# Second normalisation of the first two batches: logarithm and exponential on ScalarE, rows scaled on VectorE

## The chip, the cores and the metric

One core of a Trainium2 chip runs the whole kernel. Five engines (TensorE, VectorE, ScalarE, GpSimd and SyncE, in the profile PE, DVE, ACT, POOL and SP) each run a program of their own, in order, and meet at semaphores. The metric is the device time of one execution in microseconds; the median of several is compared. Lower is better.

## What is computed

x is 8 batches of 256 tokens of 128 values, float32. A cross attention with 8 heads of 16, then a mixture of 8 experts, two chosen for each token:

```
x = x + xattn(layernorm(x), ctx, ctx, W_Q, W_K, W_V, W_O)   # softmax over the heads' axis (axis=1)
x = x + ffn(layernorm(x), Wr, br, W1, b1, W2, b2)
layernorm(x) = (x - mean) / sqrt(var + 1e-5)
logits = x @ Wr + br;  gates = softmax over the two largest
h = relu(x @ W1[e] + b1[e]);  out = sum_e gates[e] * (h @ W2[e] + b2[e])
```

The second `layernorm` feeds the router and the experts. It is the one that the change touches.

## The kernel before

A batch's 256 tokens are two tiles (t = 0, 1) of 128 rows. The batches run through a software pipeline: while the experts of one batch run on TensorE, the scores and softmax of the next are made by VectorE and ScalarE. The attention of a batch is four units (u = 0 to 3) of 128 x 1024 scores. Every engine's order is written out by hand: `beginning()` lists the steps up to the middle of batch 1's experts one by one, and `period(i)` repeats the steady pattern after that. An engine does nothing out of this order, so a wait holds up all that stands behind it.

The steps that matter, with their lines:

- `head_max(b, u)` (VectorE, L904) takes the maximum over heads of a unit, `subtract_max` (TensorE, L344) subtracts it, `exponentiate` (ScalarE, L643) makes `e_sb`.
- `head_sum(b, u)` sums `e_sb` over the heads: on TensorE for batch 0 (L352), on GpSimd afterwards, as `half_sum`, `quarter_sum`, `e_sum` (L1156, L1158, L1161). `invert_sum` (ScalarE, L652 and L654) takes the reciprocal as a logarithm and an exponential, and `normalize` (VectorE, L912) makes `attn`.
- `add_residual(b)` (VectorE, L857) makes `x1`. `ln2(b)` (VectorE, L864 to L872) makes the mean, `ln2_var` (variance plus epsilon) and `ln2_neg`. `ln2_end(b)` (GpSimd, L1167 and L1170) makes `ln2_rstd` as a power of -0.5 and `ln2_off` = -mean * rstd. `make_x1n(b)` (ScalarE, L610) scales and shifts the two tiles into `x1n`; the profile shows it under L597, the helper `normalise`.
- `transpose_x1n` (TensorE, L283) transposes `x1n`; it waits for `x1n_made` and for the bank in `misc_ps`, for batch 1 until `k_lo(4)` has read it. `take_x1T_hi` (ScalarE, L594) and `x1T_low` (VectorE, L876) split the result into a high and a low part, and `route` (TensorE, L299) and `expert_up(b, 0)` (TensorE, L404) wait for the low part.
- `expert_up(b, e)` (L404), `relu` (ScalarE, L671), `expert_down` (TensorE, L417) and `add_expert` (VectorE, L978) run an expert. `y_ps` has two banks, so `expert_down(b, e)` waits until `add_expert(b, e - 2)` is over.

In the profile's names digits and some endings are left out: `ln2_var` and `ln1_var` are both `ln_var`, `x1` is `x`.

The orders around the change, in the lists of `beginning()`:

- VectorE, batch 0: `add_residual(0)`, `ln2(0)`, `head_max(1, 2)`, `head_max(1, 3)`, `x1T_low(0)`, `normalize(1, 0)`. Batch 1: `head_max(2, 3)`, `add_residual(1)`, `ln2(1)`, `add_expert(0, 3)`, `normalize(2, 0)`, `k_lo(4)`, `head_max(3, 0)`, `x1T_low(1)`, `add_expert(0, 4)`, `add_expert(0, 5)`, `take_logits(1)`.
- ScalarE, batch 0: `invert_sum(1, 0)`, `take_v(2)` (the profile's `v_pad`), `make_x1n(0)`, `take_x1T_hi(0)`, `exponentiate(1, 2)`, `relu(0, 0)`. Batch 1: `exponentiate(2, 2)`, `relu(0, 5)`, `invert_sum(2, 1)`, `take_k_hi(4)`, `make_x1n(1)`, `relu(0, 6)`, `take_x1T_hi(1)`.
- GpSimd: `head_sum(1, 0)`, `ln2_end(0)`, `head_sum(1, 1)` and so on; `head_sum(2, 1)`, `ln2_end(1)`, `split_w1(7)`, `head_sum(2, 2)`.
- TensorE: `transpose_x1n(0)`, `subtract_max(1, 2)`, `expert_up(0, 0)`, `scores(2, 0)`, `route(0)`. Batch 1: `expert_up(0, 6)`, `expert_down(0, 5)`, `transpose_x1n(1)`, `subtract_max(2, 3)`, `expert_up(0, 7)`, `route(1)`, `expert_down(0, 6)`.

Of the kernel before, what the change touches and what calls it, by code (L numbers as in the profile page):

```python
# [9 lines left out]
ALU = mybir.AluOpType  # L10
ACT = mybir.ActivationFunctionType
AX = mybir.AxisListType

P = 128
# [3 lines left out]
def build(nc, x, ctx_t, w_attn, wr, br, w1, b1_t, w2, b2, out):  # L18
# [3 lines left out]
    TT = S // P  # L22
# [8 lines left out]

    PERIODS = B + 5
    B2_AFTER = 2
    PE_SUMS = 4

    with ExitStack() as stack:
        def sb(name, shape, dt=F32):
            return stack.enter_context(nc.sbuf_tensor(name, shape, dt))
# [4 lines left out]
        def sem(name):  # L43
            return stack.enter_context(nc.semaphore(name))
# [47 lines left out]
        x1 = sb("x1", [P, TT, D])  # L92

        ln2_stats = sb("ln2_stats", [P, TT, 6])
        ln2_mv = sb("ln2_mv", [P, TT, 2])
        ln2_var = sb("ln2_var", [P, TT])
        ln2_rstd = sb("ln2_rstd", [P, TT])
        ln2_neg = sb("ln2_neg", [P, TT])
        ln2_off = sb("ln2_off", [P, TT])
        x1n = sb("x1n", [P, TT, D])  # L100
# [48 lines left out]
        ln2_step, ln2_var_made, ln2_neg_made, ln2_rstd_made, ln2_off_made, x1n_made = (  # L149
            sem("ln2_step"), sem("ln2_var_made"), sem("ln2_neg_made"), sem("ln2_rstd_made"), sem("ln2_off_made"),  # L150
            sem("x1n_made"))
        x1T_done, x1T_hi_made, x1T_lo_made = sem("x1T_done"), sem("x1T_hi_made"), sem("x1T_lo_made")
        logits_done, logits_step, logits_made, router_step, gap_made, gap_exp_made, gates_made = (
            sem("logits_done"), sem("logits_step"), sem("logits_made"), sem("router_step"), sem("gap_made"), sem("gap_exp_made"),
# [7 lines left out]
        def wait(eng, semaphore, n):  # L162
            if n > 0:
                eng.wait_ge(semaphore, n)
# [4 lines left out]
        def summed_on_pe(n):  # L169
            return n < PE_SUMS  # L170

# [90 lines left out]
        def _(pe):  # L262
# [125 lines left out]
            def expert_up(b, e):  # L388
# [3 lines left out]
                if j == 0:  # L392
                    pe.wait_ge(log_made, PE_SUMS)
                if b == 0:
# [196 lines left out]
        def _(act):  # L591
# [4 lines left out]
            def normalise(dst, src, off, rstd, t):  # L596
                return nc.scalar.activation(dst, src, ACT.Identity, bias=off[:, t:t + 1], scale=rstd[:, t:t + 1])  # L597
# [6 lines left out]
                op.then_inc(xn_made, 1)  # L604

            def make_x1n(b):
                act.wait_ge(ln2_off_made, b + 1)
                wait(act, x1T_done, b)
                for t in range(TT):
                    op = normalise(x1n[:, t, :], x1[:, t, :], ln2_off, ln2_rstd, t)  # L610
                op.then_inc(x1n_made, 1)
# [33 lines left out]
            def invert_sum(b, u):  # L645
# [4 lines left out]
                else:  # L650
                    act.wait_ge(sum_made, n + 1 - PE_SUMS)
                    nc.scalar.activation(log_sum[:, u, :], e_sum[:, u, :], ACT.Ln).then_inc(log_made, 1)  # L652
# [27 lines left out]
            def period(i):  # L680
                kv, coming, now, f, g, old = i, i - 1, i - 2, i - 3, i - 4, i - 5
                if there(g):
                    make_x1n(g)
# [47 lines left out]
            def beginning():  # L731
# [30 lines left out]
                invert_sum(1, 0)  # L762
                take_v(2)
                make_x1n(0)
                take_x1T_hi(0)
                exponentiate(1, 2)
# [21 lines left out]
                invert_sum(2, 1)  # L788
                take_k_hi(4)
                make_x1n(1)  # L790
                relu(0, 6)
                take_x1T_hi(1)
# [41 lines left out]
        def _(dve):  # L834
# [26 lines left out]
            def ln2(b):  # L861
                dve.wait_ge(x1_made, b + 1)
                for t in range(TT):
                    op = nc.vector.bn_stats(ln2_stats[:, t, :], x1[:, t, :])  # L864
                op.then_inc(ln2_step, 1)
                dve.wait_ge(ln2_step, 2 * b + 1)
                for t in range(TT):
                    op = nc.vector.bn_aggr(ln2_mv[:, t, :], ln2_stats[:, t, :])
                op.then_inc(ln2_step, 1)
                dve.wait_ge(ln2_step, 2 * b + 2)  # L870
                nc.vector.tensor_scalar(ln2_var[:], ln2_mv[:, :, 1], EPS, None, ALU.add).then_inc(ln2_var_made, 1)  # L871
                nc.vector.tensor_scalar(ln2_neg[:], ln2_mv[:, :, 0], -1.0, None, ALU.mult).then_inc(ln2_neg_made, 1)  # L872

            def low_part(dst, src, hi, hi_made, n, made):
# [90 lines left out]
            def add_expert(b, e):  # L965
# [3 lines left out]
                if e == 0:  # L969
                    dve.wait_ge(gates_made, b + 1)  # L970
                if e == B2_AFTER + 1:
                    dve.wait_ge(b2_added, b + 1)
# [10 lines left out]
            def add_b2(b):  # L983
                dve.wait_ge(b2_done, b + 1)
                dve.wait_ge(gated, E * b + B2_AFTER + 1)
                nc.vector.tensor_tensor(acc[:].rearrange("p t d -> p (t d)"), misc_ps[:, 0:S],
                                        acc[:].rearrange("p t d -> p (t d)"), ALU.add).then_inc(b2_added, 1)

            def period(i):
# [35 lines left out]
                if there(f):  # L1025
                    ln2(f)
# [109 lines left out]
        def _(pool):  # L1136
# [14 lines left out]
            def head_sum(b, u):  # L1151
                n = UNITS * b + u
                at = 2 * (n - PE_SUMS)
                pool.wait_ge(exp_made, n + 1)
# [7 lines left out]
                                        ALU.add).then_inc(sum_made, 1)  # L1162

            def ln2_end(b):
                pool.wait_ge(ln2_var_made, b + 1)
                wait(pool, x1n_made, b)
                nc.gpsimd.tensor_tensor(ln2_rstd[:], ln2_var[:], neg_half[:, 0:TT], ALU.pow).then_inc(ln2_rstd_made, 1)  # L1167
                pool.wait_ge(ln2_rstd_made, b + 1)
                pool.wait_ge(ln2_neg_made, b + 1)
                nc.gpsimd.tensor_tensor(ln2_off[:], ln2_neg[:], ln2_rstd[:], ALU.mult).then_inc(ln2_off_made, 1)  # L1170

            def split_w1(e):
# [93 lines left out]
```

## Time and profile before

| | us |
|---|---|
| median of 3 runs | 211.2 |
| lowest and highest of them | 210.09, 212.29 |
| the profiled execution, in all | 212.29 |
| its span, first to last instruction | 210.4 |

The span is what the profile's rows are measured in: time 0 is its start. Busy time of TensorE's matmuls is 199.6 us of it, VectorE 167.7, ScalarE 132.3, GpSimd 112.8. Matmuls are pipelined and their ends are modelled, so the first figure is no measure of TensorE at its peak. The mean granted TensorE clock is 0.992 of full speed. In a row, "L876" is a line of the kernel, `out<-in` are the tiles by name, "128x256 f32" partitions and elements in a row, and what stands in brackets is idle time of the engine just before, with what ended it.

### The profile page before, as it was taken

What the parts mean: (1) busy time and instruction counts of PE and PEld (TensorE: products, weight loads), DVE (VectorE), ACT (ScalarE), POOL (GpSimd) and SP (SyncE); (2) the same over time, 40 slices, a digit from 0 to 9 for tenths busy, and PEclk for the clock granted to TensorE, in tenths of its full rate; (3) what the DMA queues carried; (4) which work ended last, traced back from release to release, by engine and by line L of the source; (5) the groups of instructions that cost most, each with busy time, mean ns of one, the idle gap of its engine ahead of it and who ended that gap; (6) DMA issues with size and microseconds to landing.
All of it is one profiled execution on the core that took longest, in us unless ns stands there. A gap on an engine that the chain in (4) does not pass through costs nothing.

```text
span 210.4 us, 4952 instructions
## 1 busy us (share of the span) xinstructions
PE 199.6 (95%) x1736; PEld 176.7 (84%) x1736; DVE 167.7 (80%) x453; ACT 132.3 (63%) x316; POOL 112.8 (54%) x132
## 2 busy tenths in 40 slices
PE   6999977698999999999999999999999999999994
PEld 6845865596799978997999889998998899789993
DVE  6388859878798999899888988898999888556532
ACT  2227738678577856877677767587757776345441
POOL 8502838849976397719662856466746674010000
PEclk9999999979999999999999999999999999999999
DMA  6649586805605163315041503332001000000000
GB/s 182 149 121 273 145 258 183 247 4 163 171 19 166 37 174 99 94 34 154 2 153 51 171 7 121 83 126 50 3 0 28 0 2 0 28 3 2 25 3 25
DMA packets 20248, 18.70 MB, mean 89 GB/s; under 512 B 1760, under 2 KB 18688, under 8 KB 20224
## 3 DMA queue, kind: packets, MB, share of 16 engines
q1 hardware_dynamic: 17472, 16.91, 27.9%
q10 hardware_dynamic: 2752, 1.48, 2.8%
q8 instruction: 14, 0.23, 0.5%
q14 instruction: 10, 0.08, 0.1%
HBM read 11.83 MB, written 6.55 MB: 87 GB/s over the span
## 4 chain that ended last, share of the span: by engine, by line
PE 91%; DVE 3%; issue 2%; ACT 2%; POOL 1%; DVEq 0%; POOLq 0%; ACTq 0%
PE y_ps L417 28%; PE h_ps L404 22%; PE score_ps L344 7%; PE misc_ps L363 6%; PE score_ps L332 6%; PE h_ps L352 3%; PE score_ps L265 3%; PE misc_ps L384 2%; PE score_ps L321 2%; PE score_ps L404 2%; PE misc_ps L372 1%; PE misc_ps L270 1%; PE misc_ps L310 1%; PE misc_ps L289 1%; PE misc_ps L283 1%
## 5 line engine op out<-in xcount | busy, mean ns | idle before, releaser
L671 ACT ACTIVATE hT<-h_ps,b_sb 128x256 f32<-128x256 f32 x118 | 49.4, 470 | 34.1 <-PE h_ps L404 33.0
L417 PE MATMUL y_ps<-w_sb,hT 128*128 128x128 f32 x512 | 68.5, 277 | 0.0
L417 PEld LDWEIGHTS y_ps<-w_sb,hT 128*128 128x128 f32 x512 | 63.3, 191 | 3.4 <-issue 2.2
L1156 POOL TENSOR_TENSOR half_sum<-e_sb 128x512 f32<-128x512 f32 x28 | 37.2, 1328 | 32.0 <-ACT e_sb L643 31.7
L912 DVE TENSOR_TENSOR attn<-e_sb,e_rcp 128x1024 f32<-128x1024 f32 x32 | 42.2, 1321 | 3.3 <-ACT e_rcp L654 3.3
L904 DVE TENSOR_REDUCE shift_m<-score_ps 128x128 fp32r<-128x1024 f32 x32 | 38.7, 1213 | 4.0 <-PE score_ps L332 2.8
L404 PE MATMUL h_ps<-x1T_hi,w_lo 128*128 128x256 f32 x118 | 38.1, 323 | 1.3 <-ACT hT L671 0.6
L643 ACT ACTIVATE e_sb<-score_ps 128x1024 f32<-128x1024 f32 x32 | 32.8, 1024 | 5.6 <-PE score_ps L344 5.4
L978 DVE SCALAR_TENSOR_TENSOR acc<-y_ps,gates,acc 128x128 f32<-128x128 f32 x96 | 29.1, 343 | 8.6 <-PE y_ps L417 7.3
L404 PE MATMUL h_ps<-x1T_hi,w_hi 128*128 128x256 f32 x118 | 33.3, 283 | 0.0
L404 PE MATMUL h_ps<-x1T_lo,w_hi 128*128 128x256 f32 x118 | 33.3, 282 | 0.0
L1158 POOL TENSOR_TENSOR quarter_sum<-half_sum 128x256 f32<-128x256 f32 x28 | 27.5, 983 | 2.2
L404 PEld LDWEIGHTS h_ps<-x1T_hi,w_lo 128*128 128x128 f32 x118 | 22.6, 192 | 4.2 <-issue 2.0
L404 PEld LDWEIGHTS h_ps<-x1T_lo,w_hi 128*128 128x128 f32 x118 | 22.6, 192 | 0.3
L404 PEld LDWEIGHTS h_ps<-x1T_hi,w_hi 128*128 128x128 f32 x118 | 22.6, 191 | 0.0
L332 PE MATMUL score_ps<-q_stack,k_stack 128*128 128x256 f32 x112 | 20.0, 303 | 1.9 <-issue 1.9
L344 PE MATMUL score_ps<-shift_m,neg_ident 128*128 128x512 f32 x64 | 21.8, 421 | 0.0
L1161 POOL TENSOR_TENSOR e_sum<-quarter_sum 128x128 f32<-128x128 f32 x28 | 17.6, 629 | 2.2
L332 PEld LDWEIGHTS score_ps<-q_stack,k_stack 128*128 128x128 f32 x112 | 15.4, 194 | 2.4 <-issue 2.3
L1167 POOL TENSOR_TENSOR ln_rstd<-ln_var,neg_half 128x2 f32<-128x2 f32 x8 | 5.7, 707 | 21.0 <-DVE ln_var L871 21.0
L363 PE MATMUL misc_ps<-attn,v_pad 128*32 128x256 f32 x256 | 15.5, 382 | 0.6 <-issue 0.6
L344 PEld LDWEIGHTS score_ps<-shift_m,neg_ident 128*128 128x128 f32 x64 | 10.1, 193 | 3.1 <-issue 2.8
(112 smaller groups left out, 286.3 us busy)
## 6 DMA issues: line engine op xcount, KB each, us to landing
k_scratch<-k_parts SPq DMA_DIRECT2D x14, 256.0 KB, 2.6
k_stack<-k_scratch SPq DMA_DIRECT2D x14, 256.0 KB, 3.9
q_stack<-q_scratch SPq DMA_DIRECT2D x28, 128.0 KB, 2.7
q_scratch<-q_parts SPq DMA_DIRECT2D x7, 256.0 KB, 2.1
w_sb<-in_w SPq DMA_DIRECT2D x1, 1024.0 KB, 7.1
out_y<-y_out SPq DMA_DIRECT2D x8, 128.0 KB, 1.9
x_all<-in_x ACTq DMA_DIRECT2D x1, 768.0 KB, 6.1
ctxT<-in_ctx_t SPq DMA_DIRECT2D x1, 640.0 KB, 5.1
```

The costliest lines, as they stand in the source:

```text
L332: mm = nc.tensor.matmul(score_ps[:, u % 2, 2 * j * P:(2 * j + 2) * P], k_stack[:, b % 2, j, kt * P:(kt + 1) * P], q_stack[:, b % 2, j, :, ...
L344: mm = nc.tensor.matmul(score_ps[:, u % 2, half * BANK:(half + 1) * BANK], neg_ident[:], m4, start=False, stop=True, skip_group_check=True)
L363: mm = nc.tensor.matmul(misc_ps[32 * g:32 * g + 32, 0:S], v_pad[:, b % 4, kt, h, :], attn[:, b % 2, kt, h, :], start=(odd == 0 and kt == 0 ...
L404: mm = nc.tensor.matmul(hidden(j)[:, c * S:(c + 1) * S], w[:, e, c * P:(c + 1) * P], xt[:, b % 2, :], start=(k == 0), stop=(k == 2))
L417: mm = nc.tensor.matmul(y_ps[:, j % 2, t * D:(t + 1) * D], hT[:, j % 2, c, t * P:(t + 1) * P], w2_sb[:, e * HC + c, :], start=(c == 0), st ...
L643: nc.scalar.activation(e_sb[:, u, :], score_ps[:, u % 2, :], ACT.Exp, scale=SCALE).then_inc(exp_made, 1)
L671: op = nc.scalar.activation(hT[:, j % 2, c, :], hidden(j)[:, c * S:(c + 1) * S], ACT.Relu, bias=b1_sb[:, e * HC + c:e * HC + c + 1])
L904: nc.vector.tensor_reduce(shift_m[:, u % 2, :], score_ps[:, u % 2, :].rearrange("p (h q) -> p q h", h=H), AX.X, ALU.max).then_inc(max_made, 1)
L912: nc.vector.tensor_tensor(attn[:, b % 2, kt, :, qt * P:(qt + 1) * P], e_sb[:, u, :].rearrange("p (h q) -> p h q", h=H), e_rcp[:, u, :].uns ...
L978: op = nc.vector.scalar_tensor_tensor(out=dst, in0=y_ps[:, j % 2, t * D:(t + 1) * D], scalar=gates[:, b % 2, t, e:e + 1], in1=src[:, t, :] ...
L1156: nc.gpsimd.tensor_tensor(half_sum[:], e[:, 0:HQ // 2], e[:, HQ // 2:HQ], ALU.add).then_inc(sum_step, 1)
L1158: nc.gpsimd.tensor_tensor(quarter_sum[:], half_sum[:, 0:HQ // 4], half_sum[:, HQ // 4:HQ // 2], ALU.add).then_inc(sum_step, 1)
```

## The change

A constant `QUICK = 2`. For batches 0 and 1 GpSimd's `ln2_end` does nothing. ScalarE's `make_x1n` waits for the variance and makes the inverse deviation as exp(-0.5 * ln(var + eps)), on 128 x 2 values, instead of scaling the rows. VectorE, inside `ln2`, waits for it and scales the two tiles itself, as (x1 - mean) * rstd, and no longer makes `ln2_neg`. The other batches are as before, with their semaphore counts less 2. The places in the four hand-written orders are the same.

```diff
--- before.py
+++ after.py
@@ -31,6 +31,7 @@
 
     PERIODS = B + 5
     B2_AFTER = 2
+    QUICK = 2
     PE_SUMS = 4
 
     with ExitStack() as stack:
@@ -95,6 +96,7 @@
         ln2_mv = sb("ln2_mv", [P, TT, 2])
         ln2_var = sb("ln2_var", [P, TT])
         ln2_rstd = sb("ln2_rstd", [P, TT])
+        ln2_log = sb("ln2_log", [P, TT])
         ln2_neg = sb("ln2_neg", [P, TT])
         ln2_off = sb("ln2_off", [P, TT])
         x1n = sb("x1n", [P, TT, D])
@@ -149,6 +151,7 @@
         ln2_step, ln2_var_made, ln2_neg_made, ln2_rstd_made, ln2_off_made, x1n_made = (
             sem("ln2_step"), sem("ln2_var_made"), sem("ln2_neg_made"), sem("ln2_rstd_made"), sem("ln2_off_made"),
             sem("x1n_made"))
+        ln2_log_made, ln2_quick_made = sem("ln2_log_made"), sem("ln2_quick_made")
         x1T_done, x1T_hi_made, x1T_lo_made = sem("x1T_done"), sem("x1T_hi_made"), sem("x1T_lo_made")
         logits_done, logits_step, logits_made, router_step, gap_made, gap_exp_made, gates_made = (
             sem("logits_done"), sem("logits_step"), sem("logits_made"), sem("router_step"), sem("gap_made"), sem("gap_exp_made"),
@@ -604,7 +607,13 @@
                 op.then_inc(xn_made, 1)
 
             def make_x1n(b):
-                act.wait_ge(ln2_off_made, b + 1)
+                if b < QUICK:
+                    act.wait_ge(ln2_var_made, b + 1)
+                    nc.scalar.activation(ln2_log[:], ln2_var[:], ACT.Ln).then_inc(ln2_log_made, 1)
+                    act.wait_ge(ln2_log_made, b + 1)
+                    nc.scalar.activation(ln2_rstd[:], ln2_log[:], ACT.Exp, scale=-0.5).then_inc(ln2_quick_made, 1)
+                    return
+                act.wait_ge(ln2_off_made, b + 1 - QUICK)
                 wait(act, x1T_done, b)
                 for t in range(TT):
                     op = normalise(x1n[:, t, :], x1[:, t, :], ln2_off, ln2_rstd, t)
@@ -869,6 +878,14 @@
                 op.then_inc(ln2_step, 1)
                 dve.wait_ge(ln2_step, 2 * b + 2)
                 nc.vector.tensor_scalar(ln2_var[:], ln2_mv[:, :, 1], EPS, None, ALU.add).then_inc(ln2_var_made, 1)
+                if b < QUICK:
+                    dve.wait_ge(ln2_quick_made, b + 1)
+                    wait(dve, x1T_done, b)
+                    for t in range(TT):
+                        op = nc.vector.tensor_scalar(x1n[:, t, :], x1[:, t, :], ln2_mv[:, t, 0:1], ln2_rstd[:, t:t + 1],
+                                                     ALU.subtract, ALU.mult)
+                    op.then_inc(x1n_made, 1)
+                    return
                 nc.vector.tensor_scalar(ln2_neg[:], ln2_mv[:, :, 0], -1.0, None, ALU.mult).then_inc(ln2_neg_made, 1)
 
             def low_part(dst, src, hi, hi_made, n, made):
@@ -1162,11 +1179,13 @@
                                         ALU.add).then_inc(sum_made, 1)
 
             def ln2_end(b):
+                if b < QUICK:
+                    return
                 pool.wait_ge(ln2_var_made, b + 1)
                 wait(pool, x1n_made, b)
                 nc.gpsimd.tensor_tensor(ln2_rstd[:], ln2_var[:], neg_half[:, 0:TT], ALU.pow).then_inc(ln2_rstd_made, 1)
-                pool.wait_ge(ln2_rstd_made, b + 1)
-                pool.wait_ge(ln2_neg_made, b + 1)
+                pool.wait_ge(ln2_rstd_made, b + 1 - QUICK)
+                pool.wait_ge(ln2_neg_made, b + 1 - QUICK)
                 nc.gpsimd.tensor_tensor(ln2_off[:], ln2_neg[:], ln2_rstd[:], ALU.mult).then_inc(ln2_off_made, 1)
 
             def split_w1(e):
```

## Rows read from the trace of the kernel before

**Rows 1.** The chain that ended last: share of the span by engine.

```profile
PE 91%; DVE 3%; issue 2%; ACT 2%; POOL 1%; DVEq 0%; POOLq 0%; ACTq 0%
```

**Rows 2.** The same chain in order of time: start us, us, what.

```profile
36.82 0.18 DVE ln_var L871
...
37.07 0.72 POOL ln_rstd L1167
...
38.08 0.89 ACT x1n L597 x2
...
39.55 0.40 ACT x1T_hi L594
...
39.97 0.44 DVE x1T_lo L876
...
40.45 0.95 PE h_ps L404 x6
```

**Rows 3.** Timeline around batch 0: start us, us, engine line, operation, tiles.

```profile
34.82 0.73 POOL L1158 TENSOR_TENSOR quarter_sum<-half_sum 128x256 f32<-128x256 f32 x1
...
34.96 1.02 ACT L643 ACTIVATE e_sb<-score_ps 128x1024 f32<-128x1024 f32 x1 [0.27 <-PE score_ps L344]
35.09 0.48 DVE L844 TENSOR_SCALAR ln_var<-ln_mv 128x6 f32<-128x6 f32 x1
...
35.63 0.46 POOL L1161 TENSOR_TENSOR e_sum<-quarter_sum 128x128 f32<-128x128 f32 x1
...
36.78 0.38 ACT L594 ACTIVATE v_pad<-misc_ps 128x256 f32<-128x256 f32 x1
...
37.26 2.35 DVE L904 TENSOR_REDUCE shift_m<-score_ps 128x128 fp32r<-128x1024 f32 x2 [0.20 <-PE score_ps L332]
...
38.01 1.26 POOL L1156 TENSOR_TENSOR half_sum<-e_sb 128x512 f32<-128x512 f32 x1
```

**Rows 4.** Nearest operations: ns min/median/max; a pair in the timeline.

```profile
L662 ACT ACTIVATE gap_exp<-gap x8: 195/201/202, 47.9 to 194.2; 128x2 f32<-128x2 f32 x8
...
6.65 0.60 DVE L849 TENSOR_SCALAR xn<-x_all,ln_mv,ln_rstd 128x128 f32<-128x128 f32 x2 [0.83 <-POOL ln_rstd L1139]
```

**Rows 5.** Timeline, GpSimd and VectorE near 74 us.

```profile
73.21 1.94 POOL L1156 TENSOR_TENSOR half_sum<-e_sb 128x512 f32<-128x512 f32 x1 [3.51 <-ACT e_sb L643]
...
73.89 1.28 DVE L947 TENSOR_SCALAR gap_exp<-gap_exp 128x2 f32<-128x2 f32 x1
```

**Rows 6.** Timeline around batch 1.

```profile
58.75 0.45 POOL L1161 TENSOR_TENSOR e_sum<-quarter_sum 128x128 f32<-128x128 f32 x1
...
60.12 0.60 DVE L978 SCALAR_TENSOR_TENSOR acc<-y_ps,gates,acc 128x128 f32<-128x128 f32 x2
...
61.38 0.37 ACT L594 ACTIVATE k_parts<-misc_ps 128x256 fp32r<-128x256 f32 x1
...
61.85 0.42 DVE L876 TENSOR_TENSOR k_parts<-misc_ps,k_parts 128x256 fp32r<-128x256 f32 x1
...
62.19 1.22 DVE L904 TENSOR_REDUCE shift_m<-score_ps 128x128 fp32r<-128x1024 f32 x1
...
62.40 1.05 PE L417 MATMUL y_ps<-w_sb,hT 128*128 128x128 f32 x8
...
64.12 0.42 DVE L876 TENSOR_TENSOR x1T_lo<-misc_ps,x1T_hi 128x256 fp32r<-128x256 f32 x1 [0.72 <-ACT x1T_hi L594]
...
64.69 0.25 PE L299 MATMUL misc_ps<-wr_pair,x1T_hi 128*128 128x16 f32 x1
```

**Rows 7.** By stretch: busy us (PE, PEld, DVE, ACT, POOL), PEclk, DMA share, GB/s.

```profile
66.00:77.00 11.00, 11.00 (x107) 9.58 (x106) 10.76 (x26) 8.51 (x21) 6.46 (x7) 1.00 0.33 96
77.00:90.00 13.00, 13.00 (x117) 12.20 (x116) 11.79 (x31) 9.26 (x23) 9.80 (x11) 1.00 0.43 114
```

**Rows 8.** The same table: the stretch with a lower granted clock.

```profile
38.50:41.90 3.40, 2.33 (x14) 1.93 (x15) 2.85 (x3) 2.27 (x6) 2.74 (x4) 0.91 0.95 288
41.90:45.30 3.40, 3.40 (x16) 3.23 (x16) 2.73 (x12) 2.54 (x8) 2.13 (x3) 0.59 0.03 7
```

## The prediction

> **What bounds the kernel now.** I read the chain of work that ended last first. By engine it is TensorE for nine tenths of the span [rows 1]: what delays the TensorE program delays the end. Read in order of time, the same chain shows where TensorE is not its owner. Around 37 us it runs through the second normalisation of batch 0, step by step [rows 2]: VectorE makes `ln2_var` (36.82 to 36.99), GpSimd the power (37.07 to 37.8) and the offset, ScalarE the two rows (38.08 to 38.97), TensorE transposes, ScalarE takes `x1T_hi`, VectorE makes `x1T_lo` (39.97), and the first `expert_up` starts at 40.45. From 36.99 to 38.97 is 1.98 us, the stretch the change rebuilds. Then the timeline of that stretch [rows 3] says what the three engines have queued beside it: VectorE's two `head_max` of batch 1 (2.35 us together, from 37.26) fill the time in which GpSimd and ScalarE work on the normalisation. They stand between `ln2(0)` and `x1T_low(0)` in VectorE's program. The second place is batch 1, around 60 us [rows 6]; there TensorE is busy, VectorE goes from `ln_var` straight on to `add_expert(0, 3)`, and nobody waits long for x1n. Last, the table by stretches: from 66 to 77 us VectorE is busy 10.76 of 11.00 us, so what reaches it late stays late [rows 7].
>
> **What is removed.** For b = 0 and 1: one GpSimd power (0.72) and one small product, VectorE's `ln_neg` (as small as `ln_var`, 0.18, and overlapped by its neighbours, so worth at most 0.1), and two ScalarE rows (0.89 together) [rows 2]. Batches 2 to 7 keep their work; only their semaphore numbers shift, which costs nothing.
>
> **What is added.** On ScalarE a logarithm and an exponential of 128x2. Neither is in the trace in just this place, but an exponential of 128x2 is, 0.20 us [rows 4]; I take 0.20 for each, and 0.07 for each hand-over between engines or dependent instructions, which is what lies between `ln_var` and the power [rows 2]. The logarithm should cost the same to within 0.05; the kernel already runs logarithms and exponentials in turn, so no table is taken to be loaded. On VectorE two scalings of 128x128. The same instruction form was run for the first normalisation: 0.60 for two [rows 4], and this is the value I take. The change also moves something without saying so: VectorE *waits* for ScalarE inside `ln2`, and everything behind it in its program waits too.
>
> By the Trainium skill (VectorE: DVE Perf Modes, the section on the TRN2 errata) such an operation costs 58 cycles plus half its 128 columns at 0.96 GHz, an estimate of 0.13 us each. The trace has 0.60 for a pair [rows 4]; the measurement decides. By the page's price the sum below would be 2.6 instead of 3.3.
>
> **Who is in the way: GpSimd.** With `ln2_end(0)` gone GpSimd goes from `head_sum(1, 0)`, over at 36.09, at once to `head_sum(1, 1)`, whose input is ready at 35.98 [rows 3]; before, it sat waiting for `ln_var` [rows 2] and began that sum at 38.01. The trace shows what a VectorE operation that reads and writes SBUF alone does while GpSimd runs: the 128x6 `ln_var` that began at 35.09 took 0.48 and ended at 35.57, as GpSimd's `quarter_sum` ended at 35.55 [rows 3]; a 128x2 one that began at 73.89 took 1.28 and ended at 75.17, as GpSimd's `half_sum` ended at 75.15 [rows 5]; unhindered such a one takes 0.18 [rows 2]. So it is held until the GpSimd instruction ends. `ln_var` and both scalings are of that kind; the `head_max` are not seen held.
>
> By the Trainium skill (SBUF — State Buffer, Who interferes with whom) GpSimd and a VectorE tensor_scalar in a two-port mode share one port pair, and the second fully blocks; the trace agrees [rows 3, 5]. It is the rule that speaks against this change: with it the sum is 3.3, without it 2.7.
>
> **Batch 0, step by step.** `half_sum` (1.26 [rows 3]) runs from 36.10 to 37.37. `ln_var` is issued at 36.82 and held to 37.39 instead of ending at 36.99. ScalarE has finished `v_pad` at 37.16 [rows 3]: logarithm 37.46 to 37.66, exponential 37.73 to 37.93, VectorE could scale at 38.00. GpSimd's `quarter_sum` (0.73 [rows 3]) has begun at 37.45 and holds it to 38.18; two scalings less what was overlapped in the hold, about 0.5, end at 38.7. So x1n comes 0.27 before the 38.97 of the old way, but VectorE's two `head_max` begin at 38.7 instead of 37.26, end 2.35 later at 41.05, and `x1T_lo` starts then instead of at 39.97: **+1.1**. `x1T_hi`, on ScalarE, is ready long before. `subtract_max(1, 2)` and the exponential behind it also come late, but by less than that. Bounds: with no hold at all the logarithm starts at 37.2, the scalings end at 38.3 and the step is +0.7; with GpSimd's `e_sum` (0.46 [rows 3]) slipped in between the scalings, +1.6. It can't be below +0.7 while the `head_max` stand there. From 40.45 on the chain runs without a break on TensorE [rows 1, 2], so I carry the whole +1.1 to the end.
>
> **Batch 1, in the old times.** VectorE has its variance at about 60.1. ScalarE comes to its `make_x1n(1)` only after `relu(0, 5)`, `invert_sum(2, 1)` and `take_k_hi(4)`, over at 61.75 [rows 6]. Logarithm 61.8 to 62.0, exponential 62.1 to 62.3, scalings 62.34 to 62.94; GpSimd, freed at 59.20 [rows 6], is by then in the last parts of `head_sum(2, 2)`, which may hold them by up to 0.46; I take 63.1. All that time VectorE stands. `add_expert(0, 3)` starts at 63.1 instead of 60.12 (3.0 late). TensorE's `expert_down(0, 5)`, at 62.40 before, waits for it until 63.7. Behind it `normalize(2, 0)`, `k_lo(4)` and `head_max(3, 0)` take what they took, 60.12 to 63.41 or 3.29 [rows 6], to 66.4. `k_lo(4)`, at 65.25, releases the transposes, whose bank it reads; they and `x1T_hi` are over by 66.1, so VectorE's own queue is last: `x1T_lo` starts at 66.4 instead of 64.12, with 0.72 of old idle time used up [rows 6]. `route(1)`, at 64.69 before, and `expert_down(0, 6)`, which needs `add_expert(0, 4)` behind `x1T_lo`, come about **2.2** late. Bounds: 2.0 without any hold, 2.6 with a full one. Hidden at no cost: `k_lo(4)` also feeds SP's spill and load of K for batch 4, whose scores are a whole period away; and GpSimd's earlier `split_w1(7)` and sums, for which ScalarE in its order doesn't ask sooner.
>
> **Sum.** 1.1 + 2.2 = 3.3 on the profiled execution: span 210.4 to 213.7. That execution took 212.29 in all, 1.1 more than the median of the three, 211.2; I put the same 3.3 on the median: **214.5 us**. With the bounds (0.7 + 2.0 to 1.6 + 2.6) the forecast's own range is 213.9 to 215.4.
>
> **Rivals.**
> *The delay of batch 1 is absorbed.* From 60 to 77 VectorE waits little, but TensorE's busy time is a modelled one and some of it may be slack; after 77 VectorE has 1.21 us in 13 free [rows 7]. If all of 2.2 is absorbed, 1.1 stays: 212.3. Against it: VectorE is late with what TensorE must have, in a stretch where it has only 0.24 us free [rows 7].
> *The clock.* From 38.5 the granted clock falls, to 0.59 in the mean from 41.9 to 45.3 [rows 8], that is to 1.2 GHz for most of that stretch, after TensorE had waited for `x1n` and `x1T_lo`. Of 3.4 us at half speed half is lost, 1.7. The change moves TensorE's pauses there: if the fall stays away, 214.5 - 1.7 = 212.8, within 1%; this is the one by which the result would be not slower, and it decides only if the stalls are at most of the forecast size. If the longer pause brings as much slow time again, 216.2. I see no reason for either, since the pauses change place by a microsecond.
> *The shorter chain wins.* If `x1T_lo` did not stand behind the `head_max` and nothing were held, x1n at 38.3 instead of 38.97 would give -0.7 and, with ScalarE found free in batch 1, 210.5. VectorE's written order speaks against it [rows 3, 6]. The point from which it decides: scalings over by 37.3 in batch 0, before the first `head_max` has its scores.
>
> **Chances.** Forecast 0.58; absorbed 0.12; clock gained 0.10; clock lost 0.10; shorter chain 0.04; faster through something not seen 0.04, slower than all this 0.02. The range 212.6 to 216.3 leaves out the absorbed case, the shorter chain and what is unseen. About 1% (2.1 us) is what a measurement of this kernel tells from no change. Slower by more: 0.58 + 0.10 + 0.02 = 0.70. Within: 0.12 + 0.10 + 0.04 = 0.26. Faster: 0.04.
>
> **What would show it.** Right, step by step: a VectorE `ln_var` of batch 0 of some 0.6 us, ending with a GpSimd `half_sum`; logarithm and exponential of 128x2 near 0.20; scalings whose first is stretched; the `head_max` of batch 1 about 1.4 later and `x1T_lo` 1.1 later than before; near 61 to 64 us an idle VectorE of about 2 us that ScalarE's exponential ends; TensorE idle before `expert_down(0, 5)` and `route(1)`, 2 us together; and batch 2 onward the old pattern, 3.3 later. Wrong: TensorE starting its first `expert_up` near 40.45; VectorE waiting under 1 us in batch 1, which would say that ScalarE comes earlier than in its old order; the shift at 66 us shrinking toward 90; or another count of slow clock stretches.

## The result, and the profile after

The changed kernel takes 215.15 us (median of 5 runs, 214.45 to 216.89); beside it the kernel before took 210.09 (5 runs, three of them the ones above). The ratio is 1.0242, with a 95% interval of 1.0209 to 1.0275: slower by 5.1 us. The forecast was 214.5 in a range of 212.6 to 216.3, slower. It added 3.3 us to a median of 211.2, so the time came out nearer than the difference. Of all executions behind the counts below two, one of the kernel before and one of the last experiment, took 678 us at full clock, for a reason that nothing here shows; no ratio uses them. The profiled execution has a span of 214.8, against 210.4.

The timeline around batch 0 answers to [rows 2, 3]. Its columns: start and duration in us, engine, line, operation, tiles, count, and in brackets the idle time before. The kernel's lines have moved: L880 is `ln2_var`, L612 and L614 the logarithm and exponential, L885 the scalings, L893 is L876 of before, L407 is L404.

```profile
36.43 1.29 POOL L1173 TENSOR_TENSOR half_sum<-e_sb 128x512 f32<-128x512 f32 x1
...
37.20 0.55 DVE L880 TENSOR_SCALAR ln_var<-ln_mv 128x2 f32<-128x2 f32 x1
...
37.78 0.20 ACT L612 ACTIVATE ln_log<-ln_var 128x2 f32<-128x2 f32 x1 [0.23 <-DVE ln_var L880]
37.79 0.73 POOL L1175 TENSOR_TENSOR quarter_sum<-half_sum 128x256 f32<-128x256 f32 x1
38.01 0.20 ACT L614 ACTIVATE ln_rstd<-ln_log 128x2 f32<-128x2 f32 x1
38.25 0.88 DVE L885 TENSOR_SCALAR x1n<-x,ln_mv,ln_rstd 128x128 f32<-128x128 f32 x2 [0.51 <-ACT ln_rstd L614]
38.60 0.46 POOL L1178 TENSOR_TENSOR e_sum<-quarter_sum 128x128 f32<-128x128 f32 x1
39.06 2.34 DVE L921 TENSOR_REDUCE shift_m<-score_ps 128x128 fp32r<-128x1024 f32 x2
...
39.28 0.41 PE L286 MATMUL misc_ps<-ident,x1n 128*128 128x128 f32 x2 [1.20 <-DVE x1n L885]
...
40.32 0.73 PE L347 MATMUL score_ps<-shift_m,neg_ident 128*128 128x512 f32 x2 [0.63 <-DVE shift_m L921]
...
41.32 0.41 DVE L893 TENSOR_TENSOR x1T_lo<-misc_ps,x1T_hi 128x256 fp32r<-128x256 f32 x1
...
41.79 0.58 PE L407 MATMUL h_ps<-x1T_hi,w_lo 128*128 128x256 f32 x1 [0.73 <-DVE x1T_lo L893]
```

This execution stood 0.38 us later than the one of before when `add_residual(0)` ran (35.93 against 35.55), before anything of the change; times below are compared from there. `ln_var` took 0.55 and ended at 37.75 with GpSimd's `half_sum` (37.72). The pair of scalings took 0.88 and ended at 39.13, behind `e_sum` (38.60 to 39.06), which ran between them. Taken singly, the first (38.25, 0.35) was as short as an unhindered one, though `quarter_sum` ran beside it until 38.52; the second (38.52, 0.61) was the one held. The two `head_max` followed, and `x1T_lo` started 5.39 us after `add_residual(0)`; before it was 4.42 (39.97 - 35.55). The waits of TensorE in this place belong to the reading of the clock below; before they were

```profile
39.10 0.41 PE L283 MATMUL misc_ps<-ident,x1n 128*128 128x128 f32 x2 [1.41 <-ACT x1n L597]
39.27 0.71 PE L344 MATMUL score_ps<-shift_m,neg_ident 128*128 128x512 f32 x2
...
40.45 0.38 PE L404 MATMUL h_ps<-x1T_hi,w_lo 128*128 128x256 f32 x1 [0.46 <-DVE x1T_lo L876]
```

Batch 1 answers to [rows 6]:

```profile
62.61 1.18 DVE L880 TENSOR_SCALAR ln_var<-ln_mv 128x2 f32<-128x2 f32 x1
62.72 0.84 ACT L680 ACTIVATE hT<-h_ps,b_sb 128x256 f32<-128x256 f32 x2 [1.03 <-PE h_ps L407]
...
64.01 0.37 ACT L597 ACTIVATE k_parts<-misc_ps 128x256 fp32r<-128x256 f32 x1
...
64.27 0.20 ACT L612 ACTIVATE ln_log<-ln_var 128x2 f32<-128x2 f32 x1
...
64.50 0.20 ACT L614 ACTIVATE ln_rstd<-ln_log 128x2 f32<-128x2 f32 x1
...
64.74 0.72 DVE L885 TENSOR_SCALAR x1n<-x,ln_mv,ln_rstd 128x128 f32<-128x128 f32 x2 [0.95 <-ACT ln_rstd L614]
...
65.38 0.60 DVE L995 SCALAR_TENSOR_TENSOR acc<-y_ps,gates,acc 128x128 f32<-128x128 f32 x2
...
66.12 1.13 PE L420 MATMUL y_ps<-w_sb,hT 128*128 128x128 f32 x8 [0.94 <-ACT hT L680]
67.03 0.42 DVE L893 TENSOR_TENSOR k_parts<-misc_ps,k_parts 128x256 fp32r<-128x256 f32 x1
67.36 1.22 DVE L921 TENSOR_REDUCE shift_m<-score_ps 128x128 fp32r<-128x1024 f32 x1
...
67.50 0.44 PE L286 MATMUL misc_ps<-ident,x1n 128*128 128x128 f32 x2 [0.25 <-DVE k_parts L893]
...
68.49 0.42 DVE L893 TENSOR_TENSOR x1T_lo<-misc_ps,x1T_hi 128x256 fp32r<-128x256 f32 x1
...
69.05 0.25 PE L302 MATMUL misc_ps<-wr_pair,x1T_hi 128*128 128x16 f32 x1
```

VectorE did nothing between 63.79 and 64.74, and was held at the port through most of the 1.18 us before. ScalarE reached the logarithm at 64.27, behind `relu(0, 5)`, `invert_sum(2, 1)` and `take_k_hi(4)`. `add_expert(0, 3)` started 4.03 after `add_residual(1)` (61.35), against 1.40 (60.12 - 58.72); `x1T_lo` 7.14 after it, against 5.40. TensorE's `expert_down(0, 5)` at 66.12 waited for `add_expert(0, 3)`, which ended at 65.98. The bracket of its row names `hT`, but that is `relu(0, 6)`, and `expert_down(0, 5)` needs `relu(0, 5)`, done at 63.56.

Between the two, the table by stretches answers to [rows 8] (busy us of PE, PEld, DVE, ACT, POOL with instructions, granted clock, DMA share, GB/s):

```profile
38.50:41.90 3.40, 1.26 (x5) 0.61 (x5) 3.40 (x6) 1.19 (x2) 0.48 (x2) 0.91 0.84 256
41.90:45.30 3.40, 3.40 (x16) 3.40 (x17) 1.94 (x2) 1.95 (x7) 2.95 (x3) 0.50 0.20 54
45.30:48.70 3.40, 3.40 (x16) 3.03 (x15) 2.51 (x12) 1.69 (x5) 0.05 (x1) 0.58 0.02 5
48.70:52.00 3.30, 3.27 (x24) 2.75 (x23) 2.00 (x5) 2.95 (x7) 2.24 (x3) 1.00 0.47 158
```

The clock was at 1.2 GHz all through 41.9 to 45.3 and most of 45.3 to 48.7, where before only the first of these stretches was slow (0.59, and 1.00 behind it). Read in slices of 1 us, the granted clock was at half from about 41.3 to 48.1, where before it was from about 41.3 to 44.7; "a stretch" below is as much slow time as the kernel before has here. Just before, from 38.5 to 41.9, TensorE was busy for 1.26 us; before it was 2.33 [rows 8]. Part of that difference is that the whole came later. The waits in the rows above are a fairer measure: ahead of the transposes, `subtract_max(1, 2)` and the first `expert_up` TensorE stood 1.20, 0.63 and 0.73 us, 2.56 in all, against 1.41 and 0.46, 1.87 in all.

Four distances add up to the whole. They are read from the start of `add_residual` and of `x1T_lo` in each timeline, and from the span:

| us | before | changed | difference |
|---|---|---|---|
| start to `add_residual(0)` | 35.55 | 35.93 | +0.38 |
| to `x1T_lo` of batch 0 | 4.42 | 5.39 | +0.97 |
| to `add_residual(1)` | 18.75 | 20.03 | +1.28 |
| to `x1T_lo` of batch 1 | 5.40 | 7.14 | +1.74 |
| to the end | 146.3 | 146.3 | 0.0 |
| span | 210.4 | 214.8 | +4.4 |

The first row has nothing to do with the change: over all 13 profiles of this document `add_residual(0)` starts anywhere from 33.97 to 35.93. The last but one says that nothing given up by 68 us came back.

### The profile page after: what moved, and what is told of

Read it like the earlier page. It is cut to its first block, busy times and chain, and to the rows that moved or that the text cites. A ratio compares the mean times of both kernels' runs of the same rounds, so it can differ in the third digit from the quotient of the medians.

```text
span 214.8 us, 4947 instructions
## 1 busy us (share of the span) xinstructions
PE 201.7 (94%) x1736; PEld 178.0 (83%) x1736; DVE 170.1 (79%) x455; ACT 131.3 (61%) x316; POOL 108.8 (51%) x128
## 4 chain that ended last, share of the span: by engine, by line
PE 88%; DVE 6%; ACT 2%; issue 2%; POOL 0%; DVEq 0%; POOLq 0%; ACTq 0%
PE y_ps L420 27%; PE h_ps L407 21%; PE score_ps L347 7%; PE misc_ps L366 6%; PE score_ps L335 6%; PE h_ps L355 3%; PE score_ps L268 3%; PE misc_ps L387 2%; PE score_ps L324 2%; PE score_ps L407 2%; DVE shift_m L921 2%; PE misc_ps L375 1%; PE misc_ps L273 1%; DVE attn L929 1%; PE misc_ps L313 1%
## 5 line engine op out<-in xcount | busy, mean ns | idle before, releaser
L407 PE MATMUL h_ps<-x1T_hi,w_lo 128*128 128x256 f32 x118 | 38.4, 325 | 1.6 <-DVE x1T_lo L893 0.7
L407 PE MATMUL h_ps<-x1T_lo,w_hi 128*128 128x256 f32 x118 | 33.6, 285 | 0.0
L407 PE MATMUL h_ps<-x1T_hi,w_hi 128*128 128x256 f32 x118 | 33.6, 285 | 0.0
L407 PEld LDWEIGHTS h_ps<-x1T_hi,w_lo 128*128 128x128 f32 x118 | 22.8, 193 | 4.6 <-issue 2.1
L407 PEld LDWEIGHTS h_ps<-x1T_lo,w_hi 128*128 128x128 f32 x118 | 22.9, 194 | 0.3
L407 PEld LDWEIGHTS h_ps<-x1T_hi,w_hi 128*128 128x128 f32 x118 | 22.8, 193 | 0.0
L1178 POOL TENSOR_TENSOR e_sum<-quarter_sum 128x128 f32<-128x128 f32 x28 | 16.6, 594 | 2.2
L1186 POOL TENSOR_TENSOR ln_rstd<-ln_var,neg_half 128x2 f32<-128x2 f32 x6 | 4.2, 707 | 19.1 <-DVE ln_var L880 19.1
```

The lines of the kernel that those rows point to most:

```text
L407: mm = nc.tensor.matmul(hidden(j)[:, c * S:(c + 1) * S], w[:, e, c * P:(c + 1) * P], xt[:, b % 2, :], start=(k == 0), stop=(k == 2))
```

## The experiments

My theory after the result: three costs. Batch 0's queue behind the scalings (1.0), a second stretch of slow clock that TensorE's longer pause brings (1.3), and batch 1's wait of VectorE for ScalarE (1.7). The rivals: one of these carries all; the scalings or GpSimd's port, not the wait, cost the time; the clock has nothing to do with the change. Each kernel was timed beside the kernel before on the same chip. Three chips were used, so variants that were not on one chip are compared only by their ratios to it.

**The change on batch 0 alone.**

```diff
-    QUICK = 2
+    QUICK = 1
```

> The change on batch 0 alone. Theory: VectorE's two head_max start behind the scalings, so x1T_lo and the first expert_up come 1.0 us late against add_residual(0), and TensorE's longer pause there brings a second stretch of slow clock worth 1.3 us more: 2.3 us slower than before, of which the span at expert_up(0, 0) shows 1.0 and the one near 50 us 2.3. Rival A, that the cost lies in batch 1's wait: within 0.5 us of before. Rival B, that the second slow stretch has nothing to do with batch 0's pause (it depends on batch 1's or on the run): 1.0 us slower.

Ratio 1.0104 (1.0073 to 1.0135), 212.75 against 210.59 us: 2.2 slower. In its profile 5.38 us from `add_residual(0)` to `x1T_lo`, and 5.40 in batch 1, as before. So batch 0 costs what it does by itself, and rival A falls. The profile has one slow stretch and not the second one that the theory names, and 18.36 us between the batches. Rival B, the clock, needs the count of all runs (below).

**The change on batch 1 alone.**

```diff
-    QUICK = 2
+    QUICK = (1,)          # and "b in QUICK" for "b < QUICK", counts to match
```

> The change on batch 1 alone. Theory: batch 0 and the clock stay as before (one slow stretch), and the wait of VectorE for ScalarE in ln2(1) puts x1T_lo of batch 1 and all behind it 1.7 us late: 1.7 us slower than before. Rival A, that batch 0 and the clock carry all of it and batch 1's wait is absorbed: no difference. Rival B, that everything lies in batch 1: 4 to 5 us slower.

Ratio 1.0074 (1.0043 to 1.0104), 212.44 us: 1.6 slower by the ratio (1.85 between the medians). Batch 0 took 4.41, batch 1 7.14. Both rivals fall. The two parts, 1.04% and 0.74%, make 1.8% together; the whole change was 2.4% slower when first timed and 1.7% the second time (below).

**The kernel before with nothing but a wait.**

```diff
                 nc.vector.tensor_scalar(ln2_neg[:], ln2_mv[:, :, 0], -1.0, None, ALU.mult).then_inc(ln2_neg_made, 1)
+                if b == 1:
+                    dve.wait_ge(x1n_made, b + 1)
```

> The kernel before, with one wait more: VectorE waits in ln2(1) until x1n of batch 1 is made (by ScalarE, as before). No work is added or moved and GpSimd's order is the old one. Theory, that the standing VectorE is the cost in batch 1: add_expert(0, 3) starts at about 62.9 instead of 60.1 in the profile, x1T_lo of batch 1 is 1.8 us late, and the kernel 1.8 us slower than before. Rival, that the two added scalings or the port shared with GpSimd are the cost and the wait alone is absorbed: under 0.5 us.

Ratio 1.0076 (1.0045 to 1.0106), 211.82 us: as much, within these intervals, as the whole change of batch 1. The timeline of VectorE:

```profile
57.61 0.16 DVE L872 TENSOR_SCALAR ln_neg<-ln_mv 128x2 f32<-128x2 f32 x1
...
60.10 0.61 DVE L980 SCALAR_TENSOR_TENSOR acc<-y_ps,gates,acc 128x128 f32<-128x128 f32 x2 [2.33 <-ACT x1n L597]
...
63.23 0.41 DVE L878 TENSOR_TENSOR x1T_lo<-misc_ps,x1T_hi 128x256 fp32r<-128x256 f32 x1
```

It stood for 2.33 us until ScalarE's x1n was done, and `x1T_lo` came 6.95 after `add_residual(1)` instead of 5.40. So the engine that stands makes 1.55 of the 1.74 us of batch 1, with no work added.

**Idle time of TensorE filled, in the kernel before and in the changed one.** `fill(n)` issues n matmuls of `ident` into `h_ps`, which nobody reads. One cut serves for both kernels here, and its two comments say where they differ.

```diff
+                fill(4)
                 project_v(2, x1_made, 1)
...
+                fill(8)
                 transpose_x1n(0, v_taken, 3)
+                fill(4)                      # the changed kernel only
                 subtract_max(1, 2)
+                fill(4)                      # 3 in the kernel before
                 expert_up(0, 0)
```

> The kernel before with 15 idle-time matmuls of 128 columns into h_ps, which nobody reads: 4 ahead of project_v(2), 8 ahead of the transposes of x1n of batch 0 and 3 ahead of the first expert_up. Theory, that the pauses of TensorE between 35 and 41 us bring the stretch of slow clock near 42: the stretch is gone and the kernel 1.3 to 1.7 us faster. Rival, that the slow stretch doesn't hang on these pauses: the stretch stays and the time is the same within 0.5 us, or up to 0.5 slower for the matmuls.

> The changed kernel with 20 matmuls of 128 columns into h_ps that nobody reads, in TensorE's pauses between 35 and 42 us: 4 ahead of project_v(2), 8 ahead of the transposes of x1n, 4 and 4 around subtract_max(1, 2). Theory, that the longer pause brings a second stretch of slow clock: runs show on average 1 stretch fewer than the changed kernel (mean clock 0.992 or more), and the time is 1.0 to 1.7 us less than the changed kernel's. Rival, that the clock follows something else: the same clocks and a time as the changed kernel's, or a little above.

The kernel before with the fill: ratio 1.0023 (0.9993 to 1.0054), no gain. Its profile has no slow stretch and 17.58 us from `x1T_lo` to `add_residual(1)` instead of 18.75, so the clock gave 1.17 there against the one profile of the kernel before; but the fill itself made batch 0 0.29 longer, and batch 1 took 5.85 instead of 5.40, since `scores(3, 0)` started half a microsecond late in this execution; I take it that the load of Q came late, which isn't shown. And the kernel before has no slow stretch to lose in most of its runs, as the count shows; the expectation took its first profile for the rule. The changed kernel with the fill: ratio 1.0166 (1.0134 to 1.0197), 213.53 us. All its 5 runs had the full clock, and batches 0 and 1 took 5.39 and 7.17, as without it. Between them lay 17.97 us instead of 20.03. The 0.39 over the 17.58 above is the fill's own: `expert_up` started 0.87 behind `x1T_lo`, where without the last fill it is 0.47. Against the changed kernel this is 1.6 us less than its first median and 0.4 less than its second. Its table by stretches, against the one above:

```profile
41.90:45.30 3.40, 3.13 (x25) 2.94 (x24) 3.04 (x12) 3.31 (x10) 1.66 (x3) 1.00 0.22 60
45.30:48.70 3.40, 3.40 (x24) 2.70 (x22) 2.71 (x7) 2.89 (x7) 2.63 (x4) 1.00 0.39 131
```

**The changed kernel again.**

> The changed kernel unaltered, beside the others on one chip. Theory: residual to x1T_lo 5.39 and 7.1 us as in its first profile, one or two stretches of slow clock in most runs where the kernel before has none or one, 4 to 5 us slower than before. Rival, that the second slow stretch was chance in the first five runs: mostly none or one here, and 2.7 us slower than before.

Ratio 1.0169 (1.0133 to 1.0205), 213.94 us, 3.5 slower; 5.39 and 7.16 in the two batches, one slow stretch and 18.37 between them. That lies between theory and rival: the second stretch is not there every time. The waits of TensorE ahead of the fall were the same as in the first profile (1.22 and 0.63 us against 1.20 and 0.63), so they don't settle how many stretches follow.

Every run lists its mean granted clock. It falls into groups near 1.000, 0.992, 0.983 and 0.974, by the profiles none, one, two or three stretches' worth of slow clock. In each of the eight profiles that have slow clock it begins between 38.5 and 41.6 us; for the other executions the place isn't recorded. The second column is how long TensorE stood, in the kernel's profile, ahead of the transposes, `subtract_max(1, 2)` and the first `expert_up` together. (Where a second value or 2.10 stands, the clock had fallen before the last of the three waits and had shortened it.) Five of the kernels are explained below the table.

| kernel | stood, us | runs | none | one | two or three |
|---|---|---|---|---|---|
| changed (both times) | 2.56, 2.19 | 11 | 2 | 6 | 3 |
| batch 0 alone | 2.10 | 10 | 1 | 4 | 5 |
| batch 0 alone, GpSimd waits | 1.94 | 12 | 6 | 4 | 2 |
| both batches, GpSimd waits | 1.94 | 6 | 5 | 0 | 1 |
| the same, ScalarE's step moved up | 1.94 | 6 | 2 | 4 | 0 |
| ScalarE does all of it | 1.90 | 12 | 5 | 7 | 0 |
| batch 1 alone | 1.88 | 7 | 4 | 3 | 0 |
| before | 1.87 | 68 | 43 | 22 | 3 |
| before, with a wait | 1.87 | 12 | 8 | 3 | 1 |
| batch 0 alone, GpSimd waits, VectorE reordered | 1.21 | 12 | 12 | 0 | 0 |
| filled, before | | 12 | 10 | 2 | 0 |
| filled, changed | | 5 | 5 | 0 | 0 |

Kernels with the change in batch 0 and GpSimd free: 3 of 21 runs at full clock. The seven kernels that stood 1.87 to 1.94 us: 73 of 123, with much scatter between them. The one that stood 1.21: 12 of 12. Filled: 15 of 17. Within one chip, batch 0 alone had 1 of 10, where the kernel before beside it had 17 of 28.

At full clock the changed kernel took 213.1 us (2 runs) against 210.3 for the kernel before beside it: 2.8, near the 0.97 + 1.74 of the profile. By subtraction the rest of the 3.5 to 5.1 us is clock.

**GpSimd made to wait.**

```diff
                 if b < QUICK:
+                    pool.wait_ge(x1n_made, b + 1)
                     return
```

> The changed kernel, with GpSimd waiting in ln2_end(0) and (1) until VectorE has made x1n, so that it runs nothing while VectorE makes the variance and scales. Theory, that GpSimd's freed time holds VectorE up at the shared port: ln_var of batch 0 takes 0.17 instead of 0.55 and the two scalings 0.60 instead of 0.88; from add_residual(0) to x1T_lo of batch 0 it takes 5.1 us instead of 5.39 (4.42 before). In batch 1 nothing is gained, since there ScalarE is awaited. Whole kernel 0.3 us faster than the changed one. Rival, that these durations have another cause: they stay, and GpSimd's later sums make the kernel slower.

```profile
35.26 0.17 DVE L880 TENSOR_SCALAR ln_var<-ln_mv 128x2 f32<-128x2 f32 x1
...
35.97 0.60 DVE L885 TENSOR_SCALAR x1n<-x,ln_mv,ln_rstd 128x128 f32<-128x128 f32 x2 [0.54 <-ACT ln_rstd L614]
36.48 2.35 DVE L921 TENSOR_REDUCE shift_m<-score_ps 128x128 fp32r<-128x1024 f32 x2
...
38.75 0.41 DVE L893 TENSOR_TENSOR x1T_lo<-misc_ps,x1T_hi 128x256 fp32r<-128x256 f32 x1
```

`ln_var` 0.17, the pair 0.60, and 4.76 us to `x1T_lo` (38.75 - 33.99) instead of 5.39: the hold is the port, and costs 0.63, twice what I wrote there. Ratio 1.0134 (1.0103 to 1.0165). In batch 1 it is 7.26, no gain: VectorE waited 1.97 us there for ScalarE's exponential, and its `normalize(2, 0)` took 1.45 instead of 1.22 beside a `half_sum` of GpSimd that came later now and took 2.25 instead of 1.27. How much of the better time is fewer slow stretches can't be split: this kernel was not on one chip with the changed one.

**ScalarE's step moved up as well.**

```diff
+                make_x1n(1)
                 relu(0, 5)
                 invert_sum(2, 1)
                 take_k_hi(4)
-                make_x1n(1)
```

> As the one with GpSimd waiting, and ScalarE's make_x1n(1) moved up ahead of relu(0, 5). Theory, that in batch 1 VectorE stands because ScalarE's order reaches the logarithm late: VectorE's wait there shrinks from about 2 us to 0.5, and from add_residual(1) to x1T_lo of batch 1 it takes 5.9 us instead of 7.1 (5.40 before); the kernel is 1.2 us faster than the one with GpSimd waiting alone. Rival, that the delay only moves to relu(0, 5) and comes back by TensorE's expert_up(0, 6): within 0.4 us of it.

```profile
58.76 0.17 DVE L880 TENSOR_SCALAR ln_var<-ln_mv 128x2 f32<-128x2 f32 x1
...
59.44 0.60 DVE L885 TENSOR_SCALAR x1n<-x,ln_mv,ln_rstd 128x128 f32<-128x128 f32 x2 [0.51 <-ACT ln_rstd L614]
```

VectorE waited 0.51 instead of 1.97 us, and batch 1 took 5.83 instead of 7.26. Ratio 1.0092 (1.0058 to 1.0127), 0.4% under the one with GpSimd waiting alone; the two intervals overlap, so it is the profile's 1.43 us that shows the gain. In batch 1 the place in ScalarE's order was most of the price; what is left, 0.43, is the scalings and the shorter wait, less idle time that VectorE had before, and a `normalize(2, 0)` of 1.47 as above.

**Batch 0 alone, GpSimd waiting.**

> The change for batch 0 alone with GpSimd waiting until x1n is made; VectorE's order as in the changed kernel. Theory: from add_residual(0) to x1T_lo 4.76 us (4.42 before, 5.38 with the batch-0 change and GpSimd free), 0.3 us slower than before at equal clock, and fewer stretches of slow clock than the 1.5 a run of the batch-0 change with GpSimd free. Rival, that the number of slow stretches is a matter of the call and not of the kernel: as many as the changed kernel shows in this same call.

From `add_residual(0)` to `x1T_lo` 4.75 us, ratio 1.0024 (0.9994 to 1.0054), which can't be told from no change. 6 of 12 runs had the full clock; the changed kernel beside it had 2 of 6.

**The same with VectorE's order changed.**

```diff
                 head_max(1, 2)
+                x1T_low(0)
                 head_max(1, 3)
-                x1T_low(0)
```

> The change for batch 0 alone, GpSimd waiting until x1n is made, and in VectorE's order x1T_low(0) moved up between head_max(1, 2) and head_max(1, 3). Theory, that in batch 0 the cost is only the queue of VectorE behind the scalings: from add_residual(0) to x1T_lo of batch 0 it takes 4.0 us instead of 4.42 before, the first expert_up starts 0.4 us earlier, and the kernel is 0.4 us faster than before, the clock as before. Rival, that head_max(1, 3), now later, is what TensorE or VectorE miss next: within 0.2 us of before or slower.

```profile
36.53 1.22 DVE L921 TENSOR_REDUCE shift_m<-score_ps 128x128 fp32r<-128x1024 f32 x1
...
37.67 0.41 DVE L893 TENSOR_TENSOR x1T_lo<-misc_ps,x1T_hi 128x256 fp32r<-128x256 f32 x1
```

```profile
37.80 0.73 PE L347 MATMUL score_ps<-shift_m,neg_ident 128*128 128x512 f32 x2 [0.63 <-DVE shift_m L921]
...
39.74 0.70 PE L335 MATMUL score_ps<-q_stack,k_stack 128*128 128x256 f32 x4 [0.50 <-ACT e_sb L652]
```

`x1T_lo` came 3.63 after `add_residual(0)`, 0.8 earlier than before. Taking one of the two `head_max` out of its way was worth 1.12 us (4.75 less 3.63), so the queue behind the scalings was the cost of batch 0. The first `expert_up` (behind `subtract_max` at 37.80) came 4.33 after it, against 4.90 (40.45 - 35.55). But `scores(2, 0)`, next in TensorE's order, waited 0.50 us for the exponential of `subtract_max(1, 2)`, whose `head_max` still stands behind the scalings, and started 5.70 after `add_residual(0)`, as it does in the run with only a wait (39.98 - 34.27 = 5.71). The gain is given back within two microseconds; this was the rival, and the 0.4 us of the theory didn't come. All 12 runs had the full clock. Ratio 0.999 (0.997 to 1.0011): no kernel here beats the one before.

**ScalarE does all of it.**

```diff
+                    act.wait_ge(ln2_neg_made, b + 1)
...
+                    for t in range(TT):
+                        op = nc.scalar.activation(ln2_off[:, t:t + 1], ln2_neg[:, t:t + 1], ACT.Identity, scale=ln2_rstd[:, t:t + 1])
+                    op.then_inc(ln2_quick_made, 1)
...
+                    for t in range(TT):
+                        op = normalise(x1n[:, t, :], x1[:, t, :], ln2_off, ln2_rstd, t)
+                    op.then_inc(x1n_made, 1)
                     return
...
-                if b < QUICK:
-                    dve.wait_ge(ln2_quick_made, b + 1)
...
                 if b < QUICK:
+                    pool.wait_ge(ln2_neg_made, b + 1)
                     return
```

> Logarithm and exponential on ScalarE for batches 0 and 1 as in the changed kernel, but VectorE doesn't wait: it makes ln2_neg and goes on, and ScalarE makes the offset (two tiny operations) and scales the rows itself, as before. GpSimd waits only for ln2_neg. Theory, that the cost of the change is VectorE standing and scaling in front of its queue, and not the way of getting the inverse deviation: from add_residual to x1T_lo 4.4 us in batch 0 and 5.4 to 5.6 in batch 1, the kernel within 0.5 us of before. Rival, that taking the power off GpSimd costs by itself (ScalarE's four tiny operations, the shared port): 1 us slower or more.

```profile
62.82 0.42 DVE L895 TENSOR_TENSOR x1T_lo<-misc_ps,x1T_hi 128x256 fp32r<-128x256 f32 x1 [1.02 <-ACT x1T_hi L597]
```

4.43 us in batch 0 and 5.87 in batch 1, above the 5.4 to 5.6 expected; ratio 1.0037 (1.0014 to 1.0061), 0.6 us slower. Getting the deviation by logarithm and exponential costs nothing in batch 0. In batch 1 ScalarE's longer chain ends late and costs 0.5: VectorE waits 1.02 us for `x1T_hi`, where it waited 0.72 before [rows 6].

## Why the prediction was right, point by point

The direction and both queues were right, and the time came near with some luck. The forecast was +3.3 us, 2.7 to 4.2 by its own bounds; the change cost 5.1 when first timed, outside them, and 3.5 the second time. The 214.5 came within 0.7 of 215.15 because the kernel before, timed five times instead of three, had a median of 210.09 and not 211.2. The first +5.1 is what the rival "clock lost" would have given, 3.3 + 1.7.

**Batch 0, +1.1.** It was 0.97. `ln_var` was held as written (0.55; to 37.37 in the old times, that is less the 0.38 by which this execution was late, against 37.39 forecast), the logarithm and exponential took 0.20 each, and the `head_max` started 1.42 late (39.06 - 0.38 - 37.26; 1.4 forecast). What I kept for the upper bound, `e_sum` between the two scalings, did happen, and the scalings still ended at 38.75 in the old times: the hold overlapped more than I had allowed. Without any hold I had put +0.7; the kernel with GpSimd waiting shows 4.76 - 4.42 = +0.34. My sentence that it can't be below +0.7 was wrong: the scalings began 0.54 after `ln_var` and not 0.7, and I had added rows end to end. In these timelines of VectorE an instruction that doesn't wait starts some 0.1 before the one ahead of it ends (the scalings end at 36.57 there, `head_max` starts at 36.48; the two end at 38.83, `x1T_lo` starts at 38.75). So the port's share is 0.6 of the 0.97, not 0.4 of 1.1. The total was right with two terms off against each other.

By the Trainium skill (SBUF — State Buffer, Who interferes with whom) the second of two such instructions blocks; the runs agree, with 0.55 against 0.17 for the same `ln_var`. By the Trainium skill (VectorE: DVE Perf Modes, the section on the TRN2 errata) the pair of scalings would take 0.26 by estimate; it took 0.60 unhindered, as the row of before had said [rows 4].

**Batch 1, +2.2.** It was 1.74, below my lower bound of 2.0. VectorE's queue ran as written, from the scalings through `head_max(3, 0)`. Two terms were too large. The scalings came earlier: less the shift of 2.63 between the two profiles at `add_residual(1)`, the logarithm began at 61.64 and they at 62.11, where I had 61.8 and 62.34, and they were held by 0.1, where I had allowed more, so that `add_expert(0, 3)` began at 62.75 and not at 63.1. And the queue behind them, 3.11 to `x1T_lo` (68.49 - 65.38) instead of 3.29, the same end-to-end sum. Together 0.5. `add_expert(0, 3)` was 2.63 late, not 3.0; the transposes, as forecast, came with `k_lo(4)` and were not last. TensorE stood 0.94 us before `expert_down(0, 5)` and 0.25 before the transposes, 1.2 together and not the 2 that I had named as a sign; the ends of matmuls are modelled, so its busy time before may hide the rest. That `ln_var` of batch 1 would be held (1.18) I had not written down; it cost nothing, as ScalarE came later still. The rival that it is absorbed fell: 146.3 us from `x1T_lo` of batch 1 to the end in both kernels.

**The clock, 0.** This is the step that failed. I gave 0.10 to a loss of 1.7 and wrote that I saw no reason, because the pauses change place by a microsecond. They also grew, from 1.87 to 2.56 us, and in the profile a second stretch of slow clock followed: 20.03 us from `x1T_lo` to `add_residual(1)` instead of 18.75, a loss of 1.28. It also means that the forecast's own range (213.9 to 215.4) held the median for a partly wrong reason: queues 2.7 instead of 3.3, and clock on top, by subtraction 2.4 us of it the first time (5.1 - 2.7) and 0.8 the second (3.5 - 2.7).

That the longer pause brings slow stretches in the changed kernel is shown by the fill (5 of 5 runs at full clock, with both batches as slow as without it, against 2 of 11) and by batch 0 alone (1 of 10 against 17 of 28 on the same chip). For the kernel before the fill shows little: 10 of 12 against 17 of 28. It isn't shown how long or where a pause must be. The fill also kept TensorE busy from 35 us on, ahead of the pauses that the change moved, and kernels that stood equally long, about 1.9 us, had anything from 2 of 6 to 5 of 6 runs at full clock.

**What hid the rest.** SP's queue and the earlier `head_sum` and `split_w1` cost and gave nothing, as written.

## What to carry to other kernels

Before you move a step to an engine, look at what stands behind it in that engine's order: a wait inside an in-order program charges every step behind it, and in batch 1 a bare wait cost 1.55 us, nearly as much as the whole edit's 1.74. A chain can be made shorter and its end still come later; look at the last input of the next matmul, not at the end of the step you made faster. Time freed on a neighbour that shares a port comes back as holds, and in this kernel a pause of TensorE that was 0.7 us longer came with 1.28 us more of lost clock in one profile. Compare the difference with the forecast as well as the time: here the median of the kernel before moved by 1.1 us with two more runs.

## What the runs showed of the hardware

A VectorE operation of 2 columns on SBUF took 0.17 us alone, 0.55 and 1.18 while GpSimd ran, ending each time within 0.04 of GpSimd's instruction, and of a pair of scalings that let a GpSimd instruction in between its two halves the second took 0.61 instead of 0.34. `normalize`, a VectorE product of 1024 columns, and GpSimd's `half_sum` stretched each other where they ran together (1.45 and 2.25 against 1.22 and 1.27).

The number of slow clock stretches differs from run to run of one kernel: 43, 22 and 3 of 68 executions of the kernel before had none, one, and two or three. From `x1T_lo` to `add_residual(1)` it was 17.58 us with none (filled, before), 18.75 with one (before) and 20.03 with two (changed), so a stretch cost 1.2 to 1.3 there. Where a stretch began 0.9 us before `x1T_lo`, 0.8 of its cost shows there (18.37, changed again).
